# Inverting a routing table on Trainium2: one-hots by per-partition scalars in place of broadcast comparisons

## The reference

```python
raw_gate = softmax(einsum('btd,de->bte', x, gate))
_, topk_idx = top_k(raw_gate, 3)
mask = one_hot(topk_idx, 16).sum(axis=2)
gate_topk = mask * raw_gate / sum(mask * raw_gate)
hidden = relu(einsum('btd,edh->bteh', x, W1) + b1)
expert_out = einsum('bteh,ehd->bted', hidden, W2) + b2
return einsum('bte,bted->btd', gate_topk, expert_out)
```

## Time and profile before

| | us |
|---|---|
| median of 3 runs | 1821.72 (1820.7 to 1823.14) |
| the profiled execution, time | 1823.23 |
| its span in the trace | 1821.1 |
| PE busy | 1678.5 (92%) |
| DVE busy | 1392.2 (76%) |
| POOL busy | 1225.5 (67%) |
| ACT busy | 731.6 (40%) |

### The profile page before, as it was taken

One profiled execution on the slowest core, in us unless ns is written; L12 is line 12 of the kernel. 1 busy time (PEld: TensorE's weight loads), 2 busy tenths in 40 slices (PEclk: granted clock), 3 DMA queues, 4 the chain that ended last, 5 costly groups with the idle time before them and its releaser, 6 DMA issues. The chain is left out here.

```text
span 1821.1 us, 34011 instructions
## 1 busy us (share of the span) xinstructions
PE 1678.5 (92%) x9489; PEld 1260.4 (69%) x9490; DVE 1392.2 (76%) x3247; ACT 731.6 (40%) x1556; POOL 1225.5 (67%) x1051
## 2 busy tenths in 40 slices
PE   4689999999999999999999999999659999999990
PEld 3566667766666667666676666665339999999980
DVE  3568888888888888998888898887775665656655
ACT  2234454445444444445544444454352222222223
POOL 3257778777887777687876788665017777777764
PEclk9789999999999999999999999999859999999995
DMA  9976456755666777646686565541964444444448
GB/s 308 342 197 174 135 175 201 198 140 163 187 164 179 219 207 203 181 146 183 204 248 178 163 180 166 154 140 50 324 206 70 75 71 71 72 73 74 72 63 282
DMA packets 185395, 302.10 MB, mean 166 GB/s; under 512 B 23616, under 2 KB 82752, under 8 KB 185136
## 3 DMA queue, kind: packets, MB, share of 16 engines
q1 hardware_dynamic: 161888, 269.20, 49.9%
q0 software_dynamic: 21312, 30.02, 10.6%
q10 hardware_dynamic: 2064, 1.31, 0.3%
HBM read 188.67 MB, written 111.54 MB: 165 GB/s over the span
## 5 line engine op out<-in xcount | busy, mean ns | idle before, releaser
L814 ACT ACTIVATE prob<-b_ps 128x512 f32<-128x512 f32 (+3 forms) x768 | 354.6, 489 | 357.2 <-PE b_ps L613 261.1
L540 POOL TENSOR_TENSOR acc<-acc,prob 128x1024 f32<-128x1024 f32 (+1 forms) x188 | 348.3, 1853 | 6.2 <-POOL acc L540 5.2
L612 PE MATMUL b_ps<-q,k 128*128 128x512 f32 (+3 forms) x768 | 294.8, 388 | 4.9 <-ACT prob L814 3.0
L511 POOL TENSOR_TENSOR roped<-rot 128x512 f32<-128x512 f32 x128 | 174.8, 1366 | 166.6 <-DVE rot L959 165.8
L605 PE MATMUL a_ps<-k,q 128*128 128x512 f32 (+3 forms) x768 | 266.1, 383 | 19.7 <-DMA k<-scratch_hilo 9.0
L939 DVE CUSTOM_DVE_ANT_0 masked<-a_ps,causal 128x256 bf16<-128x256 f32 (+3 forms) x512 | 246.1, 496 | 45.3 <-PE a_ps L605 37.8
L695 PE MATMUL y_ps<-prob,v_sb 128*64 128x512 f32 (+3 forms) x1536 | 272.9, 490 | 0.0
L613 PE MATMUL b_ps<-q,k 65*128 65x512 f32 (+3 forms) x768 | 264.4, 348 | 0.0
L1555 POOL DMA_INDIRECT scratch_sum<-y,dst_i x111 | 184.9, 1665 | 96.0 <-ACT y L1627 95.1
L1004 DVE RECIPROCAL inv<-inv 128x128 f32<-128x128 f32 x252 | 229.1, 931 | 2.3
L516 POOL TENSOR_TENSOR lo<-roped,hi 128x512 fp32r<-128x512 f32 x128 | 176.1, 1376 | 81.1 <-ACT hi L827 81.1
(11 more groups left out here) (266 smaller groups left out, 2405.2 us busy)
## 6 DMA issues: line engine op xcount, KB each, us to landing
q<-scratch_hilo SPq DMA_DIRECT2D x192, 256.0 KB, 4.6
k<-scratch_hilo SPq DMA_DIRECT2D x192, 256.0 KB, 5.2
scratch_hilo<-hi SPq DMA_DIRECT2D x64, 512.0 KB, 4.0
scratch_hilo<-lo SPq DMA_DIRECT2D x64, 512.0 KB, 4.7
w_sb<-scratch_wsplit SPq DMA_DIRECT2D x32, 512.0 KB, 3.7
w<-in_L_ffn_W_dram SPq DMA_DIRECT2D x32, 512.0 KB, 9.6
wv_sb<-scratch_wsplit SPq DMA_DIRECT2D x16, 512.0 KB, 7.2
xT<-scratch_xsplit SPq DMA_DIRECT2D x6, 1024.0 KB, 7.6
```

The source lines that it names most:

```text
L540: nc.gpsimd.tensor_tensor(sums, old, probs(q), ALU.add).then_inc(m["sum_p"], 1)
L612: nc.tensor.matmul(out, k1[s][:, h, js], q1[s][:, h, qs], start=True, stop=False, skip_group_check=True)
L814: nc.scalar.activation(probs(q)[:, h, :], b_ps[:, h, 0:w], ACT.Exp).then_inc(exp_done[h], 1)
```

## The change

The comparisons with broadcast operands are replaced by instructions for one column each, whose compared value is a per-partition scalar (`row_of[:, c:c + 1]`). For the tiles a second per-partition scalar multiplies in the same instruction: `(ioq == tile) * part` is written straight to `coded`, and `tile_hot`, ACT's multiplication and the semaphores `r_tile` and `r_code` are gone. DVE makes three row one-hots and four coded tile one-hots per batch, ACT the fourth row one-hot in every batch. `row_of` and `tile_of` become float32.

```diff
-        row_of = sb("row_of", [P, TOPK * TILES], BF16)
-        tile_of = sb("tile_of", [P, TOPK * TILES], BF16)
+        row_of = sb("row_of", [P, TOPK * TILES], F32)
+        tile_of = sb("tile_of", [P, TOPK * TILES], F32)
...
             for a in range(BATCHES):
                 pe.wait_ge(m["r_row"], a + 1)
-                if a in SHARED:
-                    pe.wait_ge(m["r_row_a"], SHARED.index(a) + 1)
-                pe.wait_ge(m["r_code"], a + 1)
+                pe.wait_ge(m["r_row_a"], a + 1)
...
+            act.wait_ge(m["r_slots"], 1)
             for a in range(BATCHES):
-                s = a % PLACES_HOT
-                if a in SHARED:
-                    shared, last = SHARED.index(a), columns(a).start + (HOT - 1) * BLOCKS
-                    act.wait_ge(m["r_slots"], 1)
-                    if shared >= 2:
-                        act.wait_ge(m["r_row_a"], shared - 1)
-                    nc.scalar.activation(near[:, shared % 2, :], ioq[:], ACT.Square, bias=minus_row[:, last:last + 1])\
-                        .then_inc(m["r_near"], 1)
-                act.wait_ge(m["r_tile"], a + 1)
+                last = columns(a).start + (HOT - 1) * BLOCKS
+                if a >= 2:
+                    act.wait_ge(m["r_row_a"], a - 1)
+                nc.scalar.activation(near[:, a % 2, :], ioq[:], ACT.Square, bias=minus_row[:, last:last + 1])\
+                    .then_inc(m["r_near"], 1)
                 if a >= PLACES_HOT:
                     act.wait_ge(m["r_inv"], a - PLACES_HOT + 1)
-                nc.scalar.activation(coded[:, s], tile_hot[:, s], ACT.Identity,
-                                     scale=part[:, a % BLOCKS:a % BLOCKS + 1]).then_inc(m["r_code"], 1)
-                if a in SHARED:
-                    act.wait_ge(m["r_near"], shared + 1)
-                    nc.scalar.activation(row_hot[:, s, HOT - 1, :], near[:, shared % 2, :], ACT.Relu, scale=-1.0, bias=1.0)\
-                        .then_inc(m["r_row_a"], 1)
+                act.wait_ge(m["r_near"], a + 1)
+                nc.scalar.activation(row_hot[:, a % PLACES_HOT, HOT - 1, :], near[:, a % 2, :], ACT.Relu, scale=-1.0, bias=1.0)\
+                    .then_inc(m["r_row_a"], 1)
...
             for a in range(BATCHES):
-                s, some = a % PLACES_HOT, columns(a)
+                s, first = a % PLACES_HOT, columns(a).start
                 if a >= PLACES_HOT:
-                    dve.wait_ge(m["r_code"], a - PLACES_HOT + 1)
                     dve.wait_ge(m["r_inv"], a - PLACES_HOT + 1)
-                V.tensor_tensor(tile_hot[:, s], bt(ioq[:, 0:SLOT_TILES], HOT), bc(tile_of[:, some], SLOT_TILES),
-                                ALU.is_equal).then_inc(m["r_tile"], 1)
-                rows = dve_rows(a)
-                by_dve = slice(some.start, some.start + (rows - 1) * BLOCKS + 1, BLOCKS)
-                V.tensor_tensor(row_hot[:, s, 0:rows], bt(ioq[:], rows), bc(row_of[:, by_dve], P), ALU.is_equal)\
-                    .then_inc(m["r_row"], 1)
+                for i in range(HOT):
+                    c = first + i * BLOCKS
+                    if i < HOT - 1:
+                        V.tensor_scalar(row_hot[:, s, i, :], ioq[:], row_of[:, c:c + 1], None, ALU.is_equal)
+                    ins = V.tensor_scalar(coded[:, s, i, :], ioq[:, 0:SLOT_TILES], tile_of[:, c:c + 1],
+                                          part[:, a % BLOCKS:a % BLOCKS + 1], ALU.is_equal, ALU.mult)
+                ins.then_inc(m["r_row"], 1)
                 if a == 1:
                     begun_experts()
```

More of the change, by code:

```diff
@@ L1085, in routing_phase @@
         hot = early[:].rearrange("p k c -> p (k c)").bitcast(F16)
-        ends = [int(c) for c in np.cumsum([0] + [PLACES_HOT * HOT * c for c in (P, SLOT_TILES, SLOT_TILES)])]
-        row_hot, tile_hot, coded = (hot[:, ends[i]:ends[i + 1]].rearrange("p (s i c) -> p s i c", s=PLACES_HOT, i=HOT)
-                                    for i in range(3))
+        ends = [int(c) for c in np.cumsum([0] + [PLACES_HOT * HOT * c for c in (P, SLOT_TILES)])]
+        row_hot, coded = (hot[:, ends[i]:ends[i + 1]].rearrange("p (s i c) -> p s i c", s=PLACES_HOT, i=HOT)
+                          for i in range(2))
         maskb = sb("gmaskb", [P, TILES, E_], BF16)
@@ L1103, in routing_phase @@
         near = sb("near", [P, 2, P], F16)
-        SHARED = [a for a in range(BATCHES) if a % 3 < 2]
-        def dve_rows(a):
-            return HOT - 1 if a in SHARED else HOT
         unused = sb("unused", [P, SLOT_TILES], F32)
@@ L1142, in tiles_of @@
             return slice(GROUP_ORDER[i] * LG, GROUP_ORDER[i] * LG + LG)
-        names = ("r_slots r_begun r_ef r_row r_near r_row_a r_tile r_code r_inv r_stored r_w r_small r_const r_chain "
+        names = ("r_slots r_begun r_ef r_row r_near r_row_a r_inv r_stored r_w r_small r_const r_chain "
                  "r_x1 r_xtr r_xtt r_lg r_lt r_lgt r_b1 r_rs r_sub "
```

## The result

| | before | after |
|---|---|---|
| median, first comparison, us | 1822.43 (6 runs, 1820.37 to 1826.89) | 1831.45 (6 runs, 1829.35 to 1832.06) |
| ratio of after to before | | 1.0048, 95% interval 1.0036 to 1.0059 |
| median, second comparison, us | 1823.61 (16 runs) | 1829.49 (7 runs) |
| ratio, second comparison | | 1.0035, interval 1.0018 to 1.0051 |
| span of the first profiled execution, us | 1821.1 | 1829.4 |

The changed kernel is slower, by 0.35% to 0.48%. The prediction had 1828.6 us, +0.38%. The last line of the table is the part of the trace that the change touches: it is 7.40 us longer, 0.41% of 1821 us, inside both intervals.

A forecast was written before the change was run, and what follows sets the result against it. DVE was taken to bound the loop, with its change counted in full: 32.1 us for 25.17 (+7.0), less 0.1 at the tail, net +6.9 us on the 1821.72 median gives 1828.6 us (+0.38%), range 1823 to 1836.

The forecast's parts named there:

- R: In the loop, DVE's row one-hot of 128 columns with one per-partition scalar, three per batch; spacing priced at 153 ns.
- K: In the loop, DVE's coded tile of 112 columns with two per-partition scalars, four per batch; spacing priced at 220 ns.
- one scalar, two scalars: In DVE's small instructions, one per-partition scalar adds 48 ns and two add 119, not hidden by the neighbour.
- a 16-bit column: In DVE's small instructions, 2-byte columns take half of the 4-byte 0.526 ns: 33 ns for R, 29 for K.
- gain of the tail: Behind the loop, PE no longer waits for ACT's code, so the reduction starts after about 0.83 us, not 0.95.
- overlap: On DVE the next instruction starts before this one's record ends; 85 ns subtracted from each R and K.
- fixed part: Each small DVE instruction costs 157 ns before its scalars and columns, taken from copies of 1024 and 256 columns.
- A: In the loop, two-byte columns bring nothing over the copies' rate: +12.1 us net, 1833.8 us; chance 0.24.
- B: In the loop's coded tiles, the second scalar is free: K 149 ns, 1821.7 us, no change; chance 0.08.
- C: In the loop, scalars cost nothing where DVE instructions follow closely: -8.0 us net, 1813.7 us; chance 0.11.
- D: In the loop, ACT's row becomes last, Square and Relu passing 1.34 us a batch; given no chance of its own.
- hiccup of code: 120 more DVE instructions might cause a hiccup: nothing in the sum, up to +2 us at the high end; chance 0.05.

The follow-up runs named there:

- experiment 3: Kernel before with only the row one-hots built one column at a time, one scalar each; ratio to before 1.0010, loop 26.63 us.
- experiment 4: Changed kernel with the three row one-hots as one broadcast comparison again, coded tiles still one column at a time; ratio to before 1.0038, loop 33.03 us.
- experiment 5: Changed kernel with seven one-scalar one-hots per batch on DVE and the code's multiplication back on ACT; ratio 1.0011, loop 27.71 us.
- experiment 6: Changed kernel with two of each batch's four row one-hots made by ACT, two by DVE; ratio 1.0013, loop 29.60 us.
- experiment 2: Changed kernel with DVE's compared column numbers held as float32 in place of bfloat16; ratio to before 1.0054, loop 38.66 us.
- experiment 1: Changed kernel with nine groups of eight equal DVE tensor_scalar instructions added behind the loop; spacings 162 ns (128 columns, one scalar), 219 (112, two), 99 (112, immediates).
- experiment 7: Kernel before with POOL building the coded tiles of every third batch and ACT a row in every batch; ratio 1.0044, stretch from loop to reduction 36.00 us.
- experiment 8: Kernel before with POOL building every fifth batch's coded tiles in a place of their own, ACT a row in four of five; ratio 1.0035.

## Why the prediction was right

**The bound and the path.** DVE bound the loop before and after; experiments 3 to 6 each moved the loop by what their DVE instructions' spacings add up to, within 0.3 us. All 7.40 us of the stretch arrived at the gather, and the expert phase kept its length. The change is slower because it moved the multiplication by the code from an engine with some room (ACT, busy 81% of the stretch) to the one that sets the pace, where it costs a second per-partition scalar for each column.

**The prices, term by term.**

| term | predicted | measured |
|---|---|---|
| record of R, ns | 238 | 237 |
| record of K, ns | 305 | 294 |
| spacing of R, ns | 153 | 162 |
| spacing of K, ns | 220 | 219 |
| one scalar, two scalars, ns | 48, 119 | 61, 120 to 122 in the spacing |
| a 16-bit column, ns | 0.26 (estimate) | 0.27 |
| a batch, us | 1.339 | (33.53 - 0.80) / 24 = 1.364 |
| loop with experts' starts, us | 32.9 | 33.53 |
| gain of the tail, us | 0.1 | 0.16 |
| net, us | +6.9 | +7.40 |

The mis-sized term is the overlap. I had subtracted 85 ns throughout; in the loop the overlap of R is 237 - 162 = 75 ns, and that of K 294 - 219 = 75. R's spacing came out 9 ns too small by it, 0.65 us over 72 instructions, which is about the difference between the two loops. K's spacing was hit by luck in part: its record was 11 ns too high and its overlap 10 ns too high, and the two cancel. The price of one scalar was low as well, 48 ns against 61 in the spacing; R's record came out right all the same (238 against 237), so another of its parts was too high. (The fixed part comes out of its rows as 156 ns, not 157, which is worth 0.1 us.) The estimate that mattered, that 16-bit columns cost half of 4-byte ones, held; no row of before had it, and experiment 2 shows that without it the change would have cost 12.5 us.

**The rivals.** A is out by the columns (experiments 1 and 2), B by the second scalar's price (1 and 5), C by the spacings (1), and D by experiment 6, in which ACT made twice the rows and still was not last. The hiccup of code did not come: 24 batches of three R and four K at 162 and 219 ns, with 0.80 us for the experts' starts, make 33.49 us against 33.53 measured.

**The page's rule.** The page "VectorE: DVE Perf Modes" of the Trainium skill, section "The TRN2 errata", prices such an instruction at 58 cycles and, with the factor 4, a quarter of a cycle for each 16-bit column. This case comes near that for instructions without per-partition scalars: 112 columns with immediates had a spacing of 99 ns against the 90 that I estimated from it, and columns cost 0.27 ns against its 0.26. It leaves out the 61 ns of each such scalar, which here are over a third of R's spacing and over half of K's; with them the predicted gain becomes the measured loss.

**No version was faster than before.** Of six other divisions of the same work the nearest were 3 (+0.10%), 5 (+0.11%) and 6 (+0.13%). Their intervals begin at 1.0000, so their times alone hardly set them apart from before; their stretches do, by 0.61, 2.02 and 3.47 us. The division before had DVE busy for 98% of the stretch and ACT for 81%.

## What to carry to other kernels

Before an operation on several columns is split into one per column, set the spacing of the small instruction, per-partition scalars included, against the large one's time for one of its parts: here 162 to 219 ns against some 130 to 160 (0.53 us for four tiles, 0.47 for three rows). Fusing a second operation that brings a per-partition scalar is free only on an engine that is not last; here it took one instruction of 663 ns a batch from ACT and put 0.24 us of second scalars on DVE. Compare the stretch that the change touches in both traces before the spans: the spans of two traces of one kernel differed by 5.2 us, the stretch by 0.02.

## What the runs showed of the hardware

- A per-partition scalar costs a DVE `tensor_scalar` some 61 ns of spacing, the second about as much as the first (112 columns: 99, 160, 219 ns), and two cost 122 ns at 8 columns as against 120 at 112; an immediate costs nothing that can be seen (experiment 1).
- The same POOL `tensor_scalar` (128x112, two scalars) took 0.73 to 0.74 us while DVE stood idle, and the longer the more of DVE's broadcast comparisons ran beside it: 1.19 us beside two, 1.56 to 1.70 beside three, 3.77 beside six, 6.45 beside eleven (experiments 7 and 8). DVE's own records grew by at most 0.17 us beside it (0.71 against 0.54). What the two engines share there was not tested.
- Single traces of the same code start the loop up to 4.6 us apart.
